# A first mixture of experts that scatters one row per token and choice, with its later batches normalised in the next stage, and more products without use ahead of four attention stages

## The chip, the cores and the metric

The program runs on one NeuronCore of a Trainium2 chip. The metric is the time of one execution on the device in microseconds (us). It is given as the median of several executions. One execution was also recorded by the profiler, and the times of single instructions come from that one.

## What is computed

The reference is a decoder of four layers (L0 to L3) over 8 sequences of 256 tokens with 128 features, all in float32. Each layer has three parts, a self attention or a scan (`a`), an attention against a context (`x`) and a feed-forward part (`f`). After each part comes `x = layernorm(x + part(x))`, without weights. The part that the change is mostly about is L0's feed-forward part, a mixture of 8 experts in which every token picks two:

```
probs = softmax(xf @ Wg);  vals, idx = top_k(probs, 2)
w = vals / (sum(vals) + 1e-9)
for k in range(2):
    oh  = one_hot(idx[:, k], 8)
    pos = cumsum(oh, axis=0) - 1 + counts;  keep = (oh == 1) & (pos < 256)
    counts += sum(keep);  combine += w[:, k] * keep
out = sum over e of combine[:, e] * (gelu(xf @ W1[e] + b1[e]) @ W2[e] + b2[e])
```

Each expert takes at most 256 token choices, so there are 8 x 256 = 2048 slots for 4096 choices (2048 tokens, two choices each), and what finds no slot is dropped.

## The kernel before

Twelve stages run one after another in the order L0a, L0x, L0f, L1a, L1x, L1f, L2a, L2x, L2f, L3a, L3x, L3f. In every stage each engine (PE = TensorE, DVE = VectorE, ACT = ScalarE, POOL = GpSimd, SP = the queue of plain DMAs) has its own hand-written program. There is no planner: each engine walks the steps of a stage in a fixed order, and semaphores tie the engines together, so an instruction that waits holds back everything behind it on its engine. The activations stay in `x_tok` (128 lanes x 16 tiles x 128 features, two tiles per batch). The semaphore `x_done` counts the batches that are normalised, and the next stage starts on a batch when it is counted. The weights of a stage are loaded by SP when the stage before it has begun. `due(g, offset, per)` tells in which steps which batch is served.

**L0f, routing** (`L0f` of the vector engine, from L2761). The logits are in PSUM. DVE finds the first and second choice in the helper `choose` (L2775 to L2780), which compares with the maximum, multiplies by the weights `w8` of the experts, takes the maximum again and compares again. PE counts the choices ahead of each token with two products (L1484, L1485). DVE copies the counts (L2802), runs a running sum over them (L2803) and gets each choice's place in its expert. It then forms two 0/1 tables, `whose` (L2812, L2813) and `hot` (32 instructions, L2815). PE multiplies the tables (L1490, 32 products), which gives the token of every slot. Before DVE turns that into row numbers `slot_of` (L2825 to L2829), it computes the two shares of each token (L2820 to L2823).

**L0f, experts.** SP has written every batch of `x_tok` to two tensors in device memory, `x_rows` (to read from) and `sum_rows` (to add to). For each expert `e`, POOL gathers its 2 x 128 rows into `big` with two indirect DMAs (`gather`, L849). PE transposes them (`turn_slots`, L1507), multiplies by W1 (`first_layer`, L1515), ACT takes the gelu (L2156), PE multiplies by W2 (`second_layer`, L1530, L1532) and DVE scales each row by its share into `V` (`copy_y`, L2859). POOL then adds the rows to `sum_rows` with two accumulating indirect DMAs (`add_rows`, L858). An expert's add waits until that of the expert before has landed, since two experts can add to one row:

```
def add_rows(e):
    pool.wait_ge(sem(f"{n}_copied"), y_copied(e))
    if e:
        pool.wait_ge(sem(f"{n}_added"), 32 * e)
```

POOL's order is gather 0, 1, 2, 3, then add 0, gather 4, add 1, gather 5, add 2, gather 6, add 3, gather 7, add 4, 5, 6, 7. Empty slots point behind the 2048 rows: a gather leaves them out, and an add puts them into rows that nobody reads.

**L0f, end.** When all has landed, SP reads the 2048 sums back (L628, four tiles first), and DVE and POOL normalise all eight batches: `deviations` (L2874 to L2879), POOL's power for the inverse root (L873), `normed` (L2885). In L1a, PE's first step then transposes batch 0 (`turn_x`, L972) and after it computes `fold` (L957, 8 products of weights), which ACT copies (L1928). Then come V (`project_v`, L987, four chunks a batch), q and k (`project`, L1003), their rotation by DVE (L2421, L2423) and POOL (L789, L793) and the scores (L1015 to L1019). L1a has 8 heads x 8 batches = 64 steps, from step -5 on.

**The four other attention stages with 16 heads that are not clipped** (L1x, L2x, L2f, L3x; `turned_stage`) take 8 pairs of heads per batch. Their steps begin at g = -8 (L2x: -18). Before step 0, PE turns and projects the first batch and spreads the heads (`unit`, L1182). `stream_on(bank, times)` (L1351) issues products of the identity with a constant mask, of 128x128 by 128x256 in bf16, whose results are never read. They stand behind the odd steps before 0 (4 each) and behind the steps 0 to 7 (4 each; L3x only from step 3). `project_v(0)` stands at step -1.

**Constants.** POOL builds the masks of later stages in `later_consts` (L660 to L673), at the start of its L0f.

## Time and profile before

| what | value |
|---|---|
| median of 3 executions | 1880.15 us (1878.22 to 1899.85) |
| the profiled execution | 1880.75 us |
| its span, first to last instruction | 1879.0 us |
| PE busy | 1567.0 us (83%), 12643 instructions |
| DVE busy | 1290.6 us (69%), 2887 instructions |
| ACT busy | 1055.7 us (56%), 2176 instructions |
| POOL busy | 658.6 us (35%), 741 instructions |
| the chain that ended last, by engine | PE 45%, DVE 23%, POOL 10%, issue 10%, ACT 9%, DMA 2% |
| mean granted clock of PE | 0.895 of full speed |

The span is the time between the first and the last recorded instruction, and 1.75 us of the execution lie outside it. The busy times count an engine's instructions, without those that only wait or issue a plain DMA. "Issue" in the chain is time in which an engine waited for nothing that the profile shows. The granted clock is the share of TensorE's full speed that the chip let it have.

### The profile page before, as it was taken

To read this page: it belongs to the slowest core of one execution; us is meant where nothing else is said; L and a number is where in the kernel's file an instruction comes from. 1 tells how busy PE (TensorE), PEld (TensorE's weight loads), DVE (VectorE), ACT (ScalarE), POOL (GpSimd) and SP (SyncE) were. 2 spreads that over 40 slices of the span, in tenths; PEclk is the share of its full clock that TensorE was granted. 3 is DMA by queue.
4 is the path that set the end of the run, shared out by engine and by line. 5 is a ranking of instruction groups with operands and counts; after the bars stand their busy time and mean duration, and the time that the engine had idled before them with its cause. 6 is when DMAs were issued, how large, how long until landed. Compare 5 with 4: busy or idle time off the path is not lost.

```text
span 1879.0 us, 34275 instructions
## 1 busy us (share of the span) xinstructions
PE 1567.0 (83%) x12643; PEld 1117.1 (59%) x12646; DVE 1290.6 (69%) x2887; ACT 1055.7 (56%) x2176; POOL 658.6 (35%) x741
## 2 busy tenths in 40 slices
PE   6488856599997888879988899888899988978875
PEld 5344435378876555757777666555569955645542
DVE  2678862377776886579999577648844465358877
ACT  4388842176774675378787155537744440037755
POOL 1355536488884022435667223220000010001223
PEclk9699978799998899968888899999989997769985
DMA  2200121200000000000000100000000000000000
GB/s 95 108 13 13 34 86 31 45 1 1 2 1 1 2 2 2 4 34 1 1 1 1 54 2 2 2 12 1 2 2 1 1 9 1 0 18 2 2 1 23
DMA packets 13607, 28.84 MB, mean 15 GB/s; under 512 B 1505, under 2 KB 10113, under 8 KB 12545
## 3 DMA queue, kind: packets, MB, share of 16 engines
q1 hardware_dynamic: 10626, 24.55, 3.7%
q0 software_dynamic: 2816, 2.10, 0.8%
q8 instruction: 103, 1.69, 0.4%
q14 instruction: 62, 0.51, 0.1%
HBM read 21.38 MB, written 5.24 MB: 14 GB/s over the span
## 4 chain that ended last, share of the span: by engine, by line
PE 45%; DVE 23%; POOL 10%; issue 10%; ACT 9%; DMA 2%; SPq 0%; DVEq 0%; POOLq 0%; ACTq 0%
PE PS L1269 5%; DVE negmax L2504 4%; PE PS L1329 4%; POOL big L793 3%; PE PS L1562 3%; PE PS L1573 3%; DVE V L3059 3%; POOL big L781 3%; ACT big L2030 2%; ACT big L2008 2%; PE PS L1808 2%; POOL big L789 2%; PE PS L1351 2%; PE PS L1799 2%; PE PS L1274 2%
## 5 line engine op out<-in xcount | busy, mean ns | idle before, releaser
L2008 ACT ACTIVATE big<-PS 128x1024 f32<-128x1024 f32 (+1 forms) x256 | 248.4, 971 | 165.6 <-PE PS L1280 164.7
L2504 DVE TENSOR_REDUCE negmax<-PS 128x4 f32<-128x1024 f32 x192 | 235.0, 1224 | 65.9 <-PE PS L1269 64.8
L677 POOL TENSOR_TENSOR rstd<-veps,mhalf 128x2 f32<-128x2 f32 x72 | 51.8, 719 | 419.9 <-DVE veps L2392 419.5
L1269 PE MATMUL PS<-KS,QS 32*128 32x256 f32 (+1 forms) x1152 | 137.0, 324 | 54.5 <-DVE negmax L2504 40.1
L1269 PEld LDWEIGHTS PS<-KS,QS 32*128 32x128 f32 x1152 | 89.2, 192 | 133.1 <-DVE negmax L2504 92.3
L1280 PE MATMUL PS<-QS,KS 32*128 32x256 f32 (+1 forms) x1152 | 134.6, 321 | 1.4 <-ACT big L2008 1.4
L1329 PE MATMUL PS<-big,V 128*32 128x256 f32 (+1 forms) x2048 | 134.5, 381 | 0.7 <-ACT big L2008 0.4
L703 POOL TENSOR_TENSOR res<-resb,XB 128x256 f32<-128x256 f32 x24 | 17.4, 726 | 283.4 <-ACT resb L2094 283.4
L2523 DVE SCALAR_TENSOR_TENSOR QT<-PS,wint 128x1024 f32<-128x1024 f32 x64 | 77.2, 1218 | 30.1 <-PE PS L1222 30.0
L745 POOL TENSOR_SCALAR KT<-QT 128x1024 f32<-128x1024 f32 x64 | 66.7, 1042 | 68.9 <-DVE QT L2523 67.0
L1280 PEld LDWEIGHTS PS<-QS,KS 32*128 32x128 f32 x1152 | 85.2, 188 | 5.7 <-issue 3.9
L2171 ACT ACTIVATE QT<-PS,W 128x256 f32<-128x256 f32 x128 | 53.8, 471 | 60.5 <-PE PS L1562 60.5
L1325 PE MATMUL PS<-big,V 128*32 128x512 f32 x512 | 67.9, 651 | 20.9 <-ACT big L2030 11.6
L781 POOL TENSOR_SCALAR big<-big,rsum 128x256 f32<-128x256 f32 (+1 forms) x144 | 60.6, 435 | 68.9 <-DVE rsum L2439 68.9
L1708 PE MATMUL PS<-OT,SEL 16*128 16x256 f32 x256 | 72.4, 427 | 13.5 <-DVE V L3063 13.5
L793 POOL TENSOR_TENSOR big<-big 128x512 f32<-128x512 f32 x64 | 81.3, 1270 | 5.0
L1724 PE MATMUL PS<-On,V 128*128 128x128 f32 x512 | 82.0, 327 | 0.0
L2250 ACT ACTIVATE QT<-x_tok,rt 128x128 f32<-128x128 f32 x256 | 77.8, 386 | 6.9 <-PE PS L1695 4.4
L1724 PEld LDWEIGHTS PS<-On,V 128*128 128x128 f32 x512 | 75.8, 235 | 9.3 <-issue 9.2
L1329 PEld LDWEIGHTS PS<-big,V 128*32 128x32 f32 x2048 | 54.5, 111 | 45.1 <-issue 15.7
L2030 ACT ACTIVATE big<-KT,W 128x1024 f32<-128x1024 f32 x64 | 73.2, 1144 | 8.6 <-POOL KT L745 8.6
L1003 PE MATMUL PS<-OT,W 128*128 128x256 f32 x272 | 72.9, 389 | 2.4 <-ACT QT L1967 2.4
(442 smaller groups left out, 4301.6 us busy)
## 6 DMA issues: line engine op xcount, KB each, us to landing
W<-in_wpack SPq DMA_DIRECT2D x1, 4180.0 KB, 12.3
W<-in_wpack SPq DMA_DIRECT2D x1, 2560.0 KB, 8.7
W<-in_wpack SPq DMA_DIRECT2D x1, 2449.5 KB, 8.3
masks<-in_mask SPq DMA_DIRECT2D x8, 256.0 KB, 2.8
W<-in_wpack SPq DMA_DIRECT2D x1, 1538.0 KB, 6.2
x_tok<-in_x SPq DMA_DIRECT2D x1, 1024.0 KB, 4.8
ctxT<-in_ctx SPq DMA_DIRECT2D x1, 1024.0 KB, 5.9
sum_rows<-ctxT SPq DMA_DIRECT2D x1, 1024.0 KB, 4.1
```

Of the source, the lines that this page charges most:

```text
L781: ins = nc.gpsimd.tensor_scalar(PRW[:, u % 4, c0:c1], PRW[:, u % 4, c0:c1], rsum[:, u % 16, j:j + 1], 1.0, ALU.mult, ALU.mult)
L793: nc.gpsimd.tensor_tensor(q, q, RTW[:, u % 4, :, :], ALU.add).then_inc(sem("t_rope"), 1)
L1003: mm = nc.tensor.matmul(PS[:, QKB[u % 2], k * S:(k + 1) * S], w(f"{n}_w{x}", h * P, (h + 1) * P), OT[:, b, :], start=True, stop=True)
L1269: mm = nc.tensor.matmul(PS[:, MAXB[half], o], QS[r, bm % 2, tm, j * P:(j + 1) * P], KS[r, bm % 2, tm, k], start=not a.causal, stop=last)
L1280: mm = nc.tensor.matmul(PS[:, exp_banks(ge)[half], o], KS[r, be % 2, te, kb * P:(kb + 1) * P], QS[r, be % 2, te, q], start=not a.causal, s ...
L1329: mm = nc.tensor.matmul(out_rows[:, skip:S], v, PX[:, T % 2, h, kb * S:(kb + 1) * S - skip], start=first, stop=last)
L1724: mm = nc.tensor.matmul(PS[:, YB, j * P:(j + 1) * P], chunk("h", t)[:, at:at + P], by_state[:, 4 * c + k, :], start=False, stop=c == 3 and ...
L2008: nc.scalar.activation(PX[:, T % 2, 2 * p:2 * p + 2, 0:cols], PS[:, exp_banks(g)[0]:exp_banks(g)[0] + 2, 0:cols], ACT.Exp, scale=a.scale). ...
L2030: nc.scalar.activation((PX, PX2)[k][:, T % 2, 2 * p:2 * p + 2, :], clipped((QT, KT)[k], g), ACT.Exp, scale=a.scale, bias=w(("high_base", " ...
L2250: ins = nc.scalar.activation(chunk("x", t)[:, at:at + P], x_tok[:, 2 * b + j, :], ACT.Copy, scale=B_cols(b)[:, i:i + 1])
L2504: ins = nc.vector.tensor_reduce(negmax[:, h:h + 2, :].rearrange("p h j -> p (h j)"), banks.rearrange("p h (j k) -> p (h j) k", j=2), AX.X, ...
L2523: nc.vector.scalar_tensor_tensor(clipped(QT, g), PS[:, pair_banks(g):pair_banks(g) + 2, :], -100.0 / a.scale, capT[:, g // PAIRS % 2, :].u ...
```

## The change

The change does the following.

1. **Routing.** In the first choice the compare and the multiplication by `w8` become one instruction on the shifted logits. The copy of the counts (L2802) goes: PE writes them in the order in which the running sum reads them from PSUM. The second half of `whose` is formed by ACT. `slot_of` comes from two instructions, ahead of the four that compute the shares. A slot now holds a choice's number (tile, lane and which choice, 0 to 4095), and an empty slot holds 4096 or more.
2. **Scatters.** `x_rows` and the new `y_rows` have 4096 rows, `x_tok` is written to both halves of `x_rows`, and SP fills `y_rows` with zeros in L0a. `scatter` is a plain indirect DMA with a bounds check, without the wait for the expert before.
3. **Sums on chip.** SP reads both halves of `y_rows` back, two tiles of each first, then fourteen of each. POOL adds them batch by batch, all eight in L0f, and DVE adds `x_tok`.
4. **Later batches.** L0f normalises batch 0 only. Batches 1 to 7 are normalised by DVE and POOL in L1a at the steps -5, -3, -1, 1, 3, 5 and 7 and the step behind each.
5. **L1a's start.** `fold` stands ahead of `turn_x(0)` and waits for the last scatter. 12 products without use follow it.
6. **Other stages.** More products without use in L1x, L2x, L2f and L3x, and `project_v(0)` at step 0.
7. **Constants.** `later_consts` runs at the start of the program.

The diff, cut to its core:

```
-                    sp.wait_ge(ctx_loaded, 16)
-                    sp.dma_start(sum_rows[B * S:B * S + E * CAPACITY, :]..., ctxT[:, :])
+                    sp.wait_ge(consts, EARLY)
+                    sp.dma_start(y_rows.rearrange(...), zeros.unsqueeze(1).broadcast_to([P, 8, 512])).then_inc(sem("L0f_rows"), 16)
...
                     sp.wait_ge(sem("L0f_added"), 32 * E)
-                    for k, (a, b) in enumerate(((0, 4), (4, NT))):
-                        sp.dma_start(summed_in[:, a:b, :], by_lane[1][:, a:b, :])
+                    for k, (a, b) in enumerate(((0, 2), (2, NT))):
+                        sp.dma_start(y_first[:, a:b, :], y_half[0][:, a:b, :]).then_inc(sem(f"L0f_back{k}"), 16)
+                        sp.dma_start(y_second[:, a:b, :], y_half[1][:, a:b, :]).then_inc(sem(f"L0f_back{k}"), 16)
...
+            later_consts()
...
                 for s in range(W_X_AT, H * B + W_LAST):
+                    if n == "L1a" and (b := rows_due(s)) is not None:
+                        root_of_rows(b)
                     if 0 <= s - 1 < H * B:
                         norm(s - 1)
...
-                def add_rows(e):
+                def scatter(e):
                     pool.wait_ge(sem(f"{n}_copied"), y_copied(e))
-                    if e:
-                        pool.wait_ge(sem(f"{n}_added"), 32 * e)
                     for j in range(2):
-                        nc.gpsimd.indirect_dma_start(sum_rows, ..., slot_y(e)[:, j * P:(j + 1) * P], None, compute_op=ALU.add)
+                        nc.gpsimd.indirect_dma_start(y_rows, ..., slot_y(e)[:, j * P:(j + 1) * P], None,
+                                                     bounds_check=2 * B * S - 1, oob_is_err=False).then_inc(sem(f"{n}_added"), 16)
+
+                def both_choices(b):
+                    if b < 2:
+                        pool.wait_ge(sem(f"{n}_back{b}"), 32)
+                    y = y_first[:, 2 * b:2 * b + 2, :]
+                    nc.gpsimd.tensor_tensor(y, y, y_second[:, 2 * b:2 * b + 2, :], ALU.add).then_inc(sem(f"{n}_placed"), 1)
-                later_consts()
...
+                for b in range(B):
+                    both_choices(b)
+                    if b == 0:
+                        root_of_rows(b)
...
+                    if s == W_X_AT and not first:
+                        pe.wait_ge(sem("L0f_added"), 32 * E)
+                        fold()
+                        for _ in range(12):
+                            nc.tensor.matmul(PS[:, YB, 0:S], identb[:, :], causal[:, 0, :], start=True, stop=True)
                     if (b := due(s, W_X_AT, H)) is not None:
                         turn_x(b)
-                    if s == W_X_AT:
+                    if s == W_X_AT and first:
                         fold()
...
-                        if (b := due(g, a.v_at)) is not None:
+                        if (b := due(g, a.v_at)) is not None and (b or a.clip):
                             project_v(b)
...
+                        if g == 0:
+                            project_v(0)
                     if not a.clip:
                         if g < 0:
-                            stream_on(MAXB[0], 4 * (g % 2))
+                            stream_on(MAXB[0], {-7: 14, -5: 10, -3: 10, -1: 4}.get(g, 6 * (g % 2)))
+                        elif g < 4:
+                            stream_on(EXPB[0], 8)
...
-                            if n != "L3x" or g >= 3:
-                                stream_on(OUTB, 4)
+                            if g >= 4:
+                                stream_on(OUTB, 5)
...
+                act.wait_ge(sem(f"{n}_slots"), 2)
+                nc.scalar.activation(whose[:, :, 1, :], in_chunk, ACT.Copy, scale=route("lane")).then_inc(sem(f"{n}_lg"), 1)
...
                     if (b := due(s, H + W_Y_AT, H)) is not None:
                         normalise(n, b, line, (res, resb)[b % 2])
+                    if n == "L1a":
+                        if (b := rows_due(s)) is not None:
+                            moments_of_rows(b)
+                        if (b := rows_due(s - 1)) is not None:
+                            normalise_rows(b)
                     if not first and 0 <= s + 2 < H * B:
                         rotate(s + 2)
...
+                ch.step(nc.vector.scalar_tensor_tensor(found, rt[:, 0, :, :], 0.0, w8, ALU.is_equal, ALU.mult))
+                ch.step(choose(0))
...
-                ch.step(nc.vector.tensor_copy(by_expert(cnt), PS[:, 1, 0:S].rearrange("p (c e) -> p e c", e=E)))
-                ch.step(nc.vector.tensor_tensor_scan(pre, keep_on, cnt, 0.0, ALU.mult, ALU.add))
+                ch.step(nc.vector.tensor_tensor_scan(pre, keep_on, PS[:, 1, 0:S], 0.0, ALU.mult, ALU.add))
...
                 ch.step(nc.vector.tensor_tensor(prob, prob, wide(rts[:, 1, :]), ALU.mult))
+                dve.wait_ge(sem(f"{n}_counts"), 2)
+                ch.step(nc.vector.tensor_scalar(slot_share, PS[:, 7, 16:32], 2.0 * B * S, None, ALU.add))
+                nc.vector.tensor_tensor(slot_of[:, :], PS[:, 7, 0:16], slot_share, ALU.add).then_inc(sem(f"{n}_placed"), 1)
                 for k in range(2):
                     ch.step(nc.vector.tensor_tensor(scaled, prob, ohb[:, k, :, :], ALU.mult))
                     ch.step(nc.vector.tensor_reduce(rts[:, 2 + k, :], scaled, AX.X, ALU.add))
...
+            def moments_of_rows(b):
+                both_tiles = slice(2 * b, 2 * b + 2)
+                dve.wait_ge(sem("L0f_placed"), 2 + b)
+                line.step(nc.vector.tensor_tensor(y_first[:, both_tiles, :], y_first[:, both_tiles, :], x_tok[:, both_tiles, :], ALU.add))
+                for t in (2 * b, 2 * b + 1):
+                    line.did(nc.vector.bn_stats(stats_of[:, t, :], y_first[:, t, :]))
...
+            def normalise_rows(b):
+                dve.wait_ge(sem("rstd"), before("L0f", "rstd") + b + 1)
```

## Rows read from the trace of the kernel before

**Rows 1.** Chain of waits from 262 to 372 us: shares by line of this stretch.

```profile
by line: issue 26.8%; DMA sum_rows<-V,slot_of 15.6%; POOL sum_rows L858 11.1%; POOL big L849 10.0%; PE PS L987 5.0%; DVE big L2815 4.7%; PE PS L957 3.1%; DMA big<-sum_rows 2.6%; DVE x_tok L2397 1.7%; PE PS L1003 1.6%; ACT W L1928 1.0%; PE P
```

**Rows 2.** Timeline of the routing: start us, length us, engine, line, operation, out and in.

```profile
268.37 0.63 POOL L669 TENSOR_SCALAR_AFFINE_SELECT causal<-causal 128x512 bf16<-128x512 bf16 x1
268.51 0.63 DVE L2777 TENSOR_TENSOR rt<-rt,W 128x128 f32<-128x128 f32 x1
...
270.86 0.29 DVE L2777 TENSOR_TENSOR rt<-rt,W 128x128 f32<-128x128 f32 x1
...
272.56 0.42 DVE L2802 COPY big<-PS 128x256 f32<-128x256 f32 x1 [0.29 <-PE PS L1485]
...
282.76 0.40 PE L1490 MATMUL PS<-big 128*128 128x32 bf16 x8 [0.90 <-DVE big L2815]
...
284.81 0.18 DVE L2829 SCALAR_TENSOR_TENSOR slot_of<-one_more 128x16 int32<-128x16 f32 x1
```

**Rows 3.** Groups by form, 150 to 420 us: busy us, mean ns | idle before.

```profile
L858 POOL DMA_INDIRECT sum_rows<-V,slot_of x16 | 25.4, 1585 | 19.0 <-DMA sum_rows<-V,slot_of 8.2 <-DVE V L2859 7.1 <-issue 3.7
L849 POOL DMA_INDIRECT big<-x_rows,slot_of x16 | 17.0, 1064 | 21.1 <-DVE slot_of L2829 16.5 <-issue 4.3 <-DMA sum_rows<-V,slot_of 0.3
...
L694 POOL TENSOR_TENSOR XB<-x_tok,W 128x256 f32<-128x256 f32 x6 | 4.4, 733 | 0.1
```

**Rows 4.** Timeline of the experts: first result, last gather, last result.

```profile
302.86 0.61 DVE L2859 TENSOR_SCALAR V<-PS,one_more 128x128 f32<-128x128 f32 x2
...
328.53 1.04 POOL L849 DMA_INDIRECT big<-x_rows,slot_of  x1 [0.31 <-issue]
...
342.16 0.61 DVE L2859 TENSOR_SCALAR V<-PS,one_more 128x128 f32<-128x128 f32 x2 [2.39 <-PE PS L1532]
```

**Rows 5.** Pieces of the chain of waits, 262 to 372 us: start us, us, what.

```profile
350.34 3.24 DMA sum_rows<-V,slot_of
353.59 2.82 DMA big<-sum_rows
...
359.60 3.43 PE PS L957 x16
...
364.18 2.09 PE PS L987 x2
```

**Rows 6.** Timeline of L1a's start: batch 0 normalised, first rotation, first scores.

```profile
358.25 0.60 DVE L2885 TENSOR_SCALAR x_tok<-big,rt 128x128 f32<-128x128 f32 x2
...
370.91 0.69 DVE L2421 TENSOR_TENSOR big<-PS,W 128x512 f32<-128x512 f32 x1 [2.15 <-PE PS L1003]
...
375.72 0.28 PE L1015 MATMUL PS<-causal,identb 128*128 128x256 bf16 x1 [0.85 <-POOL big L793]
```

**Rows 7.** Windows: length, busy PE, PEld, DVE, ACT, POOL, granted clock, DMA share, GB/s.

```profile
440.00:467.00 27.00, 25.92 (x176) 21.73 (x176) 20.02 (x56) 19.03 (x62) 22.70 (x34) 1.00 0.00 1
610.00:615.00 5.00, 4.65 (x34) 2.83 (x35) 2.46 (x6) 2.64 (x5) 0.00 (x0) 0.50 0.00 0
1065.00:1070.00 5.00, 5.00 (x16) 3.45 (x15) 0.49 (x2) 1.20 (x3) 1.41 (x2) 0.50 0.01 3
1250.00:1255.00 5.00, 5.00 (x22) 3.24 (x21) 2.56 (x4) 0.37 (x1) 0.00 (x0) 0.50 0.00 0
1675.00:1680.00 5.00, 4.64 (x34) 2.79 (x32) 2.38 (x5) 2.29 (x3) 0.00 (x0) 0.50 0.01 3
```

**Rows 8.** Timeline of PE at the starts of L1x, L2x and L3x.

```profile
593.74 0.74 PE L1182 MATMUL PS<-HL,spread_by 32*128 32x256 f32 x8 [1.51 <-DVE HL L2562]
...
618.02 1.07 PE L1329 MATMUL PS<-big,V 128*32 128x256 f32 x16
...
1060.30 0.73 PE L1182 MATMUL PS<-HL,spread_by 32*128 32x256 f32 x8 [3.80 <-DVE QT L2584]
...
1655.88 0.73 PE L1182 MATMUL PS<-HL,spread_by 32*128 32x256 f32 x8 [1.19 <-DVE HL L2562]
...
1685.85 1.07 PE L1329 MATMUL PS<-big,V 128*32 128x256 f32 x16
```

**Rows 9.** Piece of the chain of waits, 1044 to 1075 us: products without use at half clock.

```profile
1069.36 0.85 PE PS L1351 x4
```

137 lines of the change are left out of this document (65 added, 72 removed).

## The prediction

> **What bounds the kernel now.** I read the page first: PE is busy for 83% of the span, but over stages with different limits, so I went by stretches. The chain of waits over L0f and the start of L1a [rows 1] shows what ends last there. PE has under 10% of it; 27% is issue, 16% the landing of accumulating DMAs, 21% POOL's issue of indirect DMAs. This stretch is latency: from the routing's first rows to the first scores of L1a it is 107 us [rows 2, 6]. The windows show the second thing: at the start of L1x, L2x, L2f and L3x PE is busy and runs at half clock (0.50) [rows 7], while the other engines are half idle. Everything else is left as it is by the change.
>
> **Routing.** The first choice's multiplication took 0.63 us, beside a mask instruction of POOL, and the same line took 0.29 for the second choice [rows 2]. The mask work moves to the program's start, where POOL is idle, and the multiplication is merged with its compare: -0.5 us. The copy of the counts goes: 0.42 and 0.04 until the next [rows 2], -0.46. ACT takes the second half of `whose`, some 0.26 of DVE's time. `slot_of` ends at 284.99 now; the tables' products end at 283.16 [rows 2], and with two instructions of 0.2 behind them it would be there at 283.6: -1.4. Sum: -2.6 us.
>
> **Scatters.** Now the chain goes expert by expert. POOL spends 1585 ns on an add and 1064 ns on a gather, with 0.30 between [rows 3], so a round of two adds and two gathers lasts 6.5 us; the last gather is issued at 329.57 and the last result is in `V` at 342.77, 13.2 us behind it [rows 4]. From expert 4 on each add waits for the landing of the one before (8.2 us in all [rows 3]). The last add is issued at 350.34 and has landed at 353.59 [rows 5]. The trace has no plain scatter. Upper bound: POOL's time of an add, 1.585. Then the last gather ends 2.6 earlier (327.0), the last result is there at 340.2, scatter 6 ends at 341, and the second of scatter 7 starts at 343.0 and lands at 346.2: -7.4 with the routing. Lower bound: a gather's 1.06, the nearest row, since it moves the same 128 rows of 512 bytes with a bounds check and without arithmetic. Then a round lasts 2 x 1.35 + 2 x 1.38 + 0.3 = 5.75 us. The first result is in V at 300.9 (302.86 + 0.61 - 2.6 [rows 4]), four rounds end at 324.1, the last result is there at 337.3, and the second scatter starts at 338.8 and lands at 342.0: -11.6. I take -11.6, with -7.4 as the other end.
>
> The Trainium skill ("DMA: Bandwidth & Descriptors", SWDGE vs HWDGE) says that GpSimd builds one pair of descriptors, read and write, per DMA operation. By that rule direction alone would not make a scatter dearer than a gather, which is the -11.6; by the row of the add it is -7.4.
>
> **Sums and batch 0.** The first read back took 2.82 us for 256 KB [rows 5]; two of 128 KB should take about as long. New on batch 0's path are POOL's add (a 128x256 addition is 733 ns [rows 3]) and DVE's add of x, some 0.4: +1.15 us. Batch 0 would be normalised at 358.85 [rows 6] - 11.6 + 1.15 = 348.4: -10.4. The zeros go out at 9 us, behind the loads, and nothing waits for them for 280 us: 0. The second copy of x takes the place of the writes to `sum_rows`: 0.
>
> **L1a's start.** `fold` stands between batch 0 and its V now, so the first V product starts 5.3 us behind batch 0 [rows 5, 6]. Of those, 3.43 are the fold and 1.15 ACT's copy of it. After the change both run during the read back, with the 12 products behind them: 4.6 us. A V product takes 2.09 us at half clock [rows 5], and three of them at full clock are worth another 3.1. If nothing else held it, L1a would gain 7.7 us. But something does. On DVE the first rotation now starts 12.1 us behind batch 0 and the first scores follow 4.8 us later [rows 6], and until then DVE had time for all batches. After the change DVE's first rotation stands behind batches 1 and 2, and their normalisation behind POOL's inverse root, which stands behind POOL's seven additions (7 x 0.76 = 5.3 us). Worked through: additions done 5 to 6 us behind batch 0, batch 1 normalised at 6.2 to 7.4, batch 2's moments at 8.8, its root at 9.6, normalised at 10.2, first rotation at about 10.3 and first scores at 15. That is 2 us less than the 16.9 now. Then batches 3 to 7 put 2.0 us of DVE work into every second step. In steady state DVE's 56 instructions in 27 us are eight steps with one batch's end [rows 7], so a pair of steps has 6.75 us and DVE is busy for 5.0 of them. With 2.0 more it is at 7.0: just over the period, some 0.3 us per pair, and 1 to 2 us in all where PE's early steps without values are shorter. What is gained at the front is so given back within eight steps. I take 0 for L1a from batch 0 on, between -7.7 (all of fold and clock) and +12 (C below).
>
> A rule of the skill speaks against the change here. "SBUF — State Buffer", Who interferes with whom: a DVE instruction with two SBUF inputs contends with a GpSimd instruction that reads SBUF, and who comes first holds the port for the whole instruction. The 0.63 beside POOL against 0.29 alone agrees. By the rule each of DVE's seven new additions can wait for a POOL instruction.
>
> **Products without use.** The clock is at half in all four windows [rows 7]. Four such products take 0.85 us there [rows 9], 0.21 each, and half of that at full clock. Before step 0 there are 38 instead of 16, 22 more. At full clock they are 2.4 us, and in L1x they fit where PE waits anyway (1.51 us ahead of the first `unit` [rows 8], and 0.7 behind each of two further ones). At steps 0 to 3 there are 4 more each, 0.9 us over what the waits hide, and `project_v(0)` behind the first scores gives 0.8 back. If the clock then stays up:
> L1x: from the first `unit` to the first values 593.74 to 618.02, 24.3 us [rows 8], of which four steps ran at half clock and took 10.6 us; at full clock a step is 1.9: -2.8, with the products -2.4.
> L2f: three steps at half clock, -1.8.
> L3x: 1655.88 to 1685.85, 30.0 us [rows 8]. It would be like L1x without its slow steps, 22 us: -7.5. It starts with a cold PE, on which 14 products are 2 to 3 us instead of 1.2 us of waiting, so -6.
> L2x: its clock falls in a gap of 3.80 us on DVE [rows 8], of which the products fill 1.1. Ten further products before step -7 lengthen the path by 0.9. If the clock stays up, -0.8 in the sum; if it falls all the same, +4. I take 0.
> Sum: -10.2 us, with bounds of -13 and +18 (below).
>
> **The sum** is made against the profiled execution, 1880.75 us, of which 1.75 are outside the span: -10.4 (L0f) + 0 (L1a) - 10.2 (four stages) = -20.6, so 1860 us. The median of the runs is 0.6 us below the profiled one, and I leave it at 1860. The kernel's time can be told apart from no change from about 2% on, 38 us: this gain of 1.1% is within that.
>
> **Rivals.**
> A. The plain scatter costs POOL what the add did: 4.2 us less gained, 1864. For it: both go from SBUF to device memory. Against: arithmetic and read of the target go.
> B. The clock falls in the four stages all the same, since the gaps are caused by DVE and ACT and the heads are spread by products on 32 rows only. The gain of 10.2 is gone and the products that no gap hides cost about 2: 1872. For it: the clock fell in L1x although PE was busy for most of that stretch.
> C. The later batches stall L1a. DVE waits in order for POOL's root, POOL waits in order for DVE's moments, and both contend for SBUF. Nothing of 7 x 2.0 = 14 us is hidden then, 2 us of the front remain: 1872.
> D. The other side, one mechanism: the products run at half clock and don't raise it. There are 42 more in L1x and in L2f, 54 in L3x, 51 in L2x, 189 x 0.21 = 40 us on PE, which issues in order. Waits hide at most 22 us, so +18 against -10.4: 1888. It decides from the point at which what the waits don't hide exceeds 10.4 us, about 155 products at half clock. Against it: full bf16 products are what PE did at full clock elsewhere, and 14 at a time leave little gap.
> E. L1a's front keeps all of its 7.7 us and L2x's clock stays up: 1851.
>
> **How the numbers follow.** Forecast 0.45 (1854 to 1866 by itself), A 0.15, B 0.15, C 0.10, D 0.03, E 0.12. B and C end near 1872, and both in part are likelier than one in full, so the range is 1848 to 1874. It leaves out D, B with C together and the fast tail. Faster by over 2% (below 1843) needs more than all bounds give at once (10.4 + 7.7 + 13 = 31): 0.03. Slower by over 2% needs twice D: 0.01. Within 2%: 0.96.
>
> **What would show it.** The scatters on POOL: 1.0 to 1.1 us each if the lower bound holds, 1.5 or more for A. No POOL wait on a DMA of the expert before. Last scatter landed at 340 to 344 and batch 0 normalised near 348. In L1a: PE at clock 1.00 when V starts, DVE's first rotation near 10 us behind batch 0 (15 would be C), and DVE idle before `normalise_rows` with POOL's root as the releaser. In the stages: granted clock 1.00 in the first 25 us of L1x, L2f and L3x, and 22 to 24 us from the first `unit` to the first values of L3x. The prediction is wrong if the clock rows stay at 0.50, or if L1a's length from batch 0 on changes by more than 5 us.

## The result, and the profile of the changed kernel

| what | before | changed |
|---|---|---|
| median of 13 executions each | 1880.66 us (1870.60 to 1899.85) | 1872.18 us (1865.47 to 1884.25) |
| ratio | | 0.9944, 95% interval 0.9924 to 0.9964 |
| the profiled execution | 1880.75 us | 1869.56 us |
| mean granted clock of PE | 0.895 | 0.905 |

The ratio is taken over the fast executions of both kernels, the medians over all. By the ratio the changed kernel is faster by 0.56% (0.45% by the medians), and the interval leaves out 1. The forecast of 1860 us is 12 us too low: of the 20.6 us only 8.5 came in the medians and 11.2 in the profiled executions.

The chain of waits of the changed kernel from 343 to 372 us (start us, length us, what) shows what stands behind the last scatter now, where [rows 5] had one read back and `fold`:

```profile
343.56 2.27 DMA y_rows<-V,slot_of
...
347.29 8.46 DMA big<-y_rows
...
355.83 3.04 POOL KT L876 x5
...
359.44 1.40 POOL KT L876 x2
360.84 0.67 POOL rt L893
```

The last scatter has landed at 345.83, where the last add had landed at 353.59 [rows 5]: -7.8 us. Behind it stands something that the chain of before did not have: 8.46 us in which fourteen tiles of both halves are read back, and then POOL's seven additions. This is no longer batch 0's path but that of batches 1 to 7.

The groups of POOL between 300 and 346 us answer to [rows 3] (busy us, mean ns | idle before):

```profile
L868 POOL DMA_INDIRECT y_rows<-V,slot_of x16 | 16.0, 998 | 25.1 <-DVE V L2901 19.4 <-issue 3.0 <-DVE On L2891 2.7
L861 POOL DMA_INDIRECT big<-x_rows,slot_of x8 | 8.2, 1025 | 2.4 <-issue 2.4
```

A plain scatter takes 998 ns, a gather 1025 ns here, and no scatter waits for a DMA of the expert before. The timeline of DVE and POOL (start us, length us) answers to [rows 6]:

```profile
351.72 0.60 DVE L2931 TENSOR_SCALAR x_tok<-KT,rt 128x128 f32<-128x128 f32 x2 [0.83 <-POOL rt L893]
356.69 0.83 DVE L2918 TENSOR_TENSOR KT<-KT,x_tok 128x256 f32<-128x256 f32 x1 [4.37 <-POOL KT L876]
...
361.53 0.60 DVE L2931 TENSOR_SCALAR x_tok<-KT,rt 128x128 f32<-128x128 f32 x2 [2.71 <-POOL rt L893]
...
364.27 0.60 DVE L2931 TENSOR_SCALAR x_tok<-KT,rt 128x128 f32<-128x128 f32 x2 [0.80 <-POOL rt L893]
364.79 0.68 DVE L2459 TENSOR_TENSOR big<-PS,W 128x512 f32<-128x512 f32 x1
```

Batch 0 is normalised at 352.32 (351.72 + 0.60), batches 1 and 2 at 362.13 and 364.87, and only then comes the first rotation. And the windows of the stages' starts, as in [rows 7] (the granted clock is the third number from the end):

```profile
610.00:615.00 5.00, 4.59 (x56) 3.12 (x57) 4.15 (x9) 2.82 (x5) 0.00 (x0) 1.00 0.00 0
1065.00:1070.00 5.00, 5.00 (x26) 3.72 (x25) 2.13 (x6) 0.37 (x1) 0.68 (x1) 0.50 0.00 0
1250.00:1255.00 5.00, 4.65 (x37) 3.29 (x35) 3.69 (x9) 0.99 (x3) 0.00 (x0) 1.00 0.00 0
1675.00:1680.00 5.00, 4.04 (x56) 2.51 (x56) 3.95 (x8) 3.64 (x6) 0.00 (x0) 1.00 0.01 3
```

In these windows PE runs at full clock in three of the four stages now; in L2x (1065 to 1070) it does not.

Since one execution differs from another in stretches that no edit touches, I compare stretches and not spans. The table has them for all profiled runs, each a difference of two times in the timelines. "Experts": from the first copy of a result into `V` to the last. "Scores": from `turn_x(0)` of L1a to its first scores (the product of q and k, 0.1 to 0.2 us behind the one with the mask). "Steps": from there to L1a's first batch being normalised. "Rest": from there to L1x's first `turn_x`. L1a as a whole is the sum of these three. The fronts go from a stage's first `turn_x` to its first `values`. "Other": the sum of all stretches between the fronts and to the last product.

| run | experts | scores | steps | rest | L1x | L2x | L2f | L3x | other |
|---|---|---|---|---|---|---|---|---|---|
| before | 39.3 | 16.9 | 39.2 | 174.7 | 28.3 | 41.9 | 27.5 | 35.3 | 1148.5 |
| changed | 41.8 | 17.1 | 44.2 | 173.9 | 25.6 | 46.2 | 25.5 | 28.6 | 1146.9 |
| e12, changed again | 40.0 | 17.0 | 44.3 | 174.1 | 25.6 | 43.0 | 25.5 | 28.4 | 1153.7 |
| e1, L0f part only | 35.7 | 16.7 | 44.2 | 173.9 | 28.4 | 41.4 | 31.5 | 36.2 | 1142.7 |
| e2, products only | 41.5 | 16.6 | 39.2 | 174.4 | 25.6 | 42.9 | 25.5 | 28.7 | 1138.3 |
| e3 | 35.5 | 9.6 | 43.6 | 179.6 | 25.6 | 41.5 | 25.5 | 28.7 | 1144.7 |
| e4 | 35.6 | 12.2 | 45.0 | 174.9 | 25.6 | 41.4 | 25.5 | 28.3 | 1146.5 |
| e5 | 35.6 | 9.6 | 42.5 | 179.8 | 25.6 | 41.5 | 25.5 | 28.6 | 1144.9 |
| e6 | 37.1 | 9.6 | 42.7 | 180.3 | 25.6 | 41.5 | 25.5 | 28.7 | 1146.0 |
| e7 | 35.7 | 13.0 | 42.7 | 181.2 | 25.6 | 46.3 | 25.5 | 28.7 | 1145.7 |
| e8 | 35.6 | 25.5 | 40.6 | 174.5 | 25.6 | 46.3 | 25.5 | 28.3 | 1151.6 |
| e9 | 35.5 | 16.6 | 45.2 | 167.2 | 25.6 | 40.1 | 25.5 | 28.3 | 1151.6 |
| e10 | 35.5 | 9.6 | 45.1 | 172.9 | 25.6 | 41.5 | 25.5 | 28.7 | 1145.7 |
| e11 | 35.4 | 12.2 | 46.0 | 167.2 | 25.6 | 40.1 | 25.5 | 28.3 | 1151.6 |

The last column holds nothing that the runs change on purpose, and it moves by 15 us between them. Much of that goes with the clock: the stretch from L2f's first `values` to L3x's first `turn_x` takes 369 us at a mean granted clock of 0.95 (e7) and 389 us at 0.90 (e12). So a median of a few runs says little on 5 us, and a stretch says much.

Two things must be kept apart from what an edit does. The medians of the kernel before, taken beside the runs, are 1880.8 us for e1 to e4, 1888.7 for e5 to e8, 1888.1 for e9 to e11 and 1884.5 for e12, so across these groups only the ratios can be compared. And in all variants of the changed kernel but e12 the experts take 35 to 37 us instead of 41.8, which makes their profiled execution shorter by 5 to 6 us whatever was edited in L1a.

### The profile page after: what moved, and what is told of

The parts are those of the page before. It is cut to its first block, busy times and chain, and to the rows that moved or that the text cites. A ratio compares the mean times of both kernels' runs of the same rounds, so it can differ in the third digit from the quotient of the medians.

```text
span 1867.8 us, 34707 instructions
## 1 busy us (share of the span) xinstructions
PE 1581.1 (85%) x12844; PEld 1135.7 (61%) x12847; DVE 1295.2 (69%) x2889; ACT 1055.6 (57%) x2177; POOL 651.8 (35%) x750
## 4 chain that ended last, share of the span: by engine, by line
PE 47%; DVE 23%; POOL 11%; issue 9%; ACT 8%; DMA 2%; SPq 0%; DVEq 0%; POOLq 0%; ACTq 0%
PE PS L1294 5%; PE PS L1354 4%; DVE negmax L2547 4%; POOL big L803 4%; DVE V L3099 3%; PE PS L1596 3%; PE PS L1607 3%; POOL big L791 3%; PE PS L1376 3%; ACT big L2066 2%; POOL big L799 2%; PE PS L1299 2%; ACT big L2044 2%; PE PS L1350 2%; PE PS L1368 2%
## 5 line engine op out<-in xcount | busy, mean ns | idle before, releaser
L1294 PE MATMUL PS<-KS,QS 32*128 32x256 f32 (+1 forms) x1152 | 135.4, 320 | 50.3 <-DVE negmax L2547 37.1
L1354 PE MATMUL PS<-big,V 128*32 128x256 f32 (+1 forms) x2048 | 139.1, 392 | 0.7 <-ACT big L2044 0.4
L1758 PE MATMUL PS<-On,V 128*128 128x128 f32 x512 | 89.8, 348 | 0.8 <-DVE V L3103 0.8
L1758 PEld LDWEIGHTS PS<-On,V 128*128 128x128 f32 x512 | 83.3, 255 | 10.3 <-issue 9.3
L1376 PE MATMUL PS<-causal,identb 128*128 128x256 bf16 x595 | 85.9, 287 | 0.0
L1350 PE MATMUL PS<-big,V 128*32 128x512 f32 x512 | 67.7, 649 | 20.9 <-ACT big L2066 11.6
L1742 PE MATMUL PS<-OT,SEL 16*128 16x256 f32 x256 | 70.5, 418 | 11.6 <-DVE V L3103 11.6
```

The source lines that it names most:

```text
L1294: mm = nc.tensor.matmul(PS[:, MAXB[half], o], QS[r, bm % 2, tm, j * P:(j + 1) * P], KS[r, bm % 2, tm, k], start=not a.causal, stop=last)
L1350: mm = nc.tensor.matmul(out_rows.rearrange("p (k c) -> p k c", k=2), v, PX_BOTH[:, :, T % 2, h, kb * S:(kb + 1) * S], start=first, stop=last)
L1354: mm = nc.tensor.matmul(out_rows[:, skip:S], v, PX[:, T % 2, h, kb * S:(kb + 1) * S - skip], start=first, stop=last)
L1376: nc.tensor.matmul(PS[:, bank, 0:S], identb[:, :], causal[:, 0, :], start=True, stop=True)
L1758: mm = nc.tensor.matmul(PS[:, YB, j * P:(j + 1) * P], chunk("h", t)[:, at:at + P], by_state[:, 4 * c + k, :], start=False, stop=c == 3 and ...
```

## The experiments

### The two halves of the change

e1 takes the products and `project_v` of the four stages back, e2 puts only them into the kernel before:

```
-                        if g < 0:
-                            stream_on(MAXB[0], {-7: 14, -5: 10, -3: 10, -1: 4}.get(g, 6 * (g % 2)))
-                        elif g < 4:
-                            stream_on(EXPB[0], 8)
+                        if g < 0:
+                            stream_on(MAXB[0], 4 * (g % 2))
```

> The changed kernel with the products without use and project_v(0) as in the kernel before. Theory (the L0f part nets nothing: it gains 6.5 us until batch 0 is normalised and loses 5 us from there to L1a's steady steps): 1879 to 1881 us, L1a's first batch normalised at 413 to 414 us in the trace, the front of L1x back at 28 us and of L3x at 34 to 36 us. Rival (the L0f part is worth what was forecast for it, about 10 us, and the products nothing): 1870 us. A second rival is that the clock's later dips move the end by 5 us either way whatever is changed; then this run and the next do not add up to the whole change.

> The kernel before with only the products without use and project_v(0) of the change. Theory (all of the gain is theirs: -2.7 in L1x, -1.8 in L2f, -6.6 in L3x, +4.3 in L2x, and what later dips give): 1870 to 1873 us; front of L1x (first transposition to first values) 25 to 26 us against 28.3, of L3x 28 to 29 against 35.3, of L2x 46 against 41.9. Rival (they are worth nothing by themselves and the L0f part brings the gain): 1880 us with the fronts at their old lengths.

e1: median 1875.0 us, ratio 0.9952 (0.9896 to 1.0007). e2: median 1872.9 us, ratio 0.9925 (0.9868 to 0.9982); one of its six executions took 3532.7 us, and the ratio leaves it out. The intervals cannot part the theory from its rival for e1, but the stretches can. With the products taken back, L1x's front is at 28.4 and L3x's at 36.2 us again; with them alone these are 25.6 and 28.7. The gain in the fronts of L1x, L2f and L3x is the products'. L1a's steps take 44.2 us in e1 and 39.2 in e2, as in the changed kernel and in the one before: the 5 us lost there belong to the L0f part. My first theory for e1, that the L0f part nets nothing, was too low: the experts take 35.7 us in e1 and not 41.8. The ratios of the two halves, 0.48% and 0.75% of gain, add up to more than the 0.56% of the whole, as the second rival of e1 had it: the experts and L2x's front are both at their long values in the changed kernel.

### L1a's start: which work stands ahead of the first rotation

e3 does the later batches once in eight steps, both additions on DVE, from a tile that L1a leaves alone:

```
 def rows_due(s):
-    b, rest = divmod(s - W_X_AT, 2)
-    return b + 1 if rest == 0 and b + 1 < B else None
+    b, rest = divmod(s, 8)
+    return b + 1 if s >= 0 and rest == 0 and b + 1 < B else None
...
-                for b in range(B):
-                    both_choices(b)
-                    if b == 0:
-                        root_of_rows(b)
+                both_choices(0)
+                root_of_rows(0)
```

> The changed kernel, but batches 1 to 7 are added up, and normalised, once in eight steps of L1a (moments at the steps 0, 8, 16 up to 48), both additions on DVE, with the second choice's rows read back to a tile that L1a does not use; POOL adds for batch 0 alone. Theory (L1a lost its lead since batch 1 waits for 8.5 us of read back and DVE's first rotation stands behind batches 1 and 2, and then POOL and DVE contend): first rotation 5 to 7 us behind batch 0 instead of 12.5, first scores 10 to 12 behind it instead of 16.9, L1a's first batch normalised 6 to 8 us earlier than in the changed kernel (405 to 408), and 1863 to 1867 us. Rival (V's start on PE and ACT bounds the front, not the rows): first scores still 15 or more behind batch 0, time as the changed kernel's 1872.

Median 1858.5 us, ratio 0.9898 (0.9846 to 0.9950). The timeline of e3, DVE and then PE:

```profile
347.28 0.60 DVE L2933 TENSOR_SCALAR x_tok<-KT,rt 128x128 f32<-128x128 f32 x2 [0.90 <-POOL rt L891]
352.89 0.69 DVE L2457 TENSOR_TENSOR big<-PS,W 128x512 f32<-128x512 f32 x1 [5.00 <-PE PS L1021]
...
356.25 1.39 DVE L2917 TENSOR_TENSOR KT<-KT,QS 128x256 f32<-128x256 f32 x1
```

```profile
357.41 0.28 PE L1033 MATMUL PS<-causal,identb 128*128 128x256 bf16 x1 [0.93 <-POOL big L803]
```

The first rotation waits for PE's q and k and for nothing else, and it starts 5.0 us behind batch 0; the first scores come at 9.6 instead of 17.1. L1a's first batch is normalised 53.2 us behind batch 0 and not 61.2. The theory holds for the front. But it left out the other side: a round of eight steps now takes 27.6 us instead of 26.45, and of the 7.5 us gained at the front L1a's rest gives 5.7 back. L1a as a whole is 2.4 us shorter than in the changed kernel; most of e3's gain in time is in the experts (6.3) and in L2x's front (4.7).

e4 leaves the work where the change put it and only lets it start earlier: the read back in parts of two, four and ten tiles, POOL's additions one at a time behind its roots.

```
-                    for k, (a, b) in enumerate(((0, 2), (2, NT))):
+                    for k, (a, b) in enumerate(((0, 2), (2, 6), (6, NT))):
```

> The changed kernel, but the read back goes in three parts (two, four, ten tiles of each half), POOL adds batches 0, 1 and 2 ahead of L1a and the others behind its inverse roots in L1a, one at a time. Batches are normalised at the same steps as in the changed kernel. Theory (what holds the front is the 8.5 us of read back, then POOL's seven additions in a row ahead of the first root): second read back landed 3 to 4 us behind its issue, batch 1 normalised at 355 to 357 instead of 361.5, first rotation 8 to 9 us behind batch 0 instead of 12.5, L1a's first batch normalised 3 to 4 us earlier, 1868 us. Rival (DVE's own work for batches 1 and 2 beside POOL is what holds it): first rotation 11 or more behind batch 0 and no gain.

Median 1863.3 us, ratio 0.9900 (0.9853 to 0.9947). The chain of e4:

```profile
344.89 0.72 POOL rt L897
345.61 1.40 POOL KT L893 x2
347.00 0.42 DVE KT L2922
```

POOL adds batches 1 and 2 right behind batch 0's root, 10.2 us earlier than in the changed kernel (355.83), of which 6.0 are the scatters' earlier landing. The first rotation starts 7.7 us behind batch 0, the first scores come at 12.2 instead of 17.1. So 4.9 of the 7.5 us that e3 gains at the front were the waiting for fourteen tiles and the seven additions in a row; e4 changes both at once and does not tell them apart. The timeline of DVE in e4 shows what is left:

```profile
354.79 0.69 DVE L2463 TENSOR_TENSOR big<-PS,W 128x512 f32<-128x512 f32 x1 [1.74 <-PE PS L1027]
```

The rotation waits 1.74 us for PE's q and k; the first V product took 2.05 us in this run, at half clock, in spite of the 12 products. DVE's rows are not what ends this wait any more.

e8 goes the other way and normalises all eight batches in L0f, as the kernel before did:

```
                 moments_of_rows(0)
                 normalise_rows(0)
+                for b in range(1, B + 1):
+                    if b < B:
+                        moments_of_rows(b)
+                    if b > 1:
+                        normalise_rows(b - 1)
```

> The changed kernel, but all eight batches are normalised in L0f, as in the kernel before, and none in L1a. Theory (moving the later batches into L1a was not what cost; the late read back and DVE's work ahead of the first rotation were, and here all of that work stands ahead of it): first rotation 17 to 20 us behind batch 0, first scores 22 to 25, L1a's first batch normalised 62 to 64 us behind batch 0 (the changed kernel 61.9, before 56.8), time 1872 to 1876. Rival (the move itself costs, through POOL's roots and DVE's port in the first steps): 57 to 59 us and 1868.

Median 1873.2 us, ratio 0.9924 (0.9889 to 0.9960). First scores 25.5 us behind batch 0, L1a's first batch 66.2 behind it, more than expected. The whole of L1a (scores, steps, rest) takes 240.6 us against 235.1 in the changed kernel and 230.8 before. The move into L1a was right: with these sums on chip it saves 5 us. What costs is that the sums are there so late.

e8 also helps to find the 5.0 us that L1a's steps lost. PE's timelines have them at one place, between the first scores and the fifth:

| | first to fifth scores | fifth to thirteenth |
|---|---|---|
| before | 11.7 us | 25.8 us |
| changed (and e1, e12) | 16.7 us | 25.9 us |
| e8 | 13.2 us | 25.8 us |

From the first rotation to the fifth scores the windows are, before and changed (busy PE, PEld, DVE, ACT, POOL):

```profile
370.91:387.40 16.49, 13.73 (x72) 9.49 (x71) 13.53 (x32) 11.66 (x34) 12.70 (x18) 0.98 0.03 10
364.79:385.90 21.11, 13.26 (x65) 9.69 (x65) 19.85 (x57) 10.94 (x33) 14.89 (x21) 0.84 0.01 2
```

DVE is busy for 19.85 of 21.11 us in the changed kernel, against 13.53 of 16.49 before, and POOL waits for it (changed kernel, POOL):

```profile
377.46 0.84 POOL L791 TENSOR_SCALAR big<-big,rsum 128x128 f32<-128x128 f32 x2 [1.64 <-DVE rsum L2477]
```

In this stretch stand the moments of batches 3, 4 and 5. Batches 6 and 7 come behind the fifth scores, beside steps of 3.5 us with a V product on PE, and there the moments and roots cost 0.1 us in eight steps. Without later batches in L1a (e8) the first stretch is 3.4 us shorter than in the changed kernel. What makes up the other 1.5 us against the kernel before is not shown. The clock may have a part: it is granted at 0.84 in this stretch against 0.98 before, though PE is busy for only 13.26 of the 21.11 us.

e7 takes the 12 products behind `fold` away (from e5, which is shown below):

```
                         fold()
-                        for _ in range(12):
-                            nc.tensor.matmul(PS[:, YB, 0:S], identb[:, :], causal[:, 0, :], start=True, stop=True)
```

> e5_late_gap without the 12 products behind fold at L1a's start. Theory (fold alone does not bring the clock up before V starts): a V product 2.1 us instead of 1.1, first rotation 7 to 8 us behind batch 0 instead of 5, first scores 12 to 13 instead of 9.6, +2 to +3 us. Rival (fold's 3.8 us of work bring the clock up anyway, or q and k and not V set the first rotation): first scores at 10 or less and the same time as e5_late_gap.

Median 1869.8 us, ratio 0.9884 (0.9806 to 0.9961). V's first product takes 2.05 us at half clock instead of 1.10, the first rotation comes at 8.0 and the first scores at 13.0. The prediction's 3.1 us for V at full clock is right in size: 3.4 at the scores. The products don't always bring it: of the eleven profiles that have them, V's first product is at 1.10 in eight and at 1.92 to 2.05 in e4, e9 and e11.

### What sets L1a's pace

e5 moves the moments of the later batches into the gap of DVE ahead of L1a's own normalise:

```
+                    if n == "L1a" and (b := rows_due(s)) is not None:
+                        moments_of_rows(b)
                     if (b := due(s, H + W_Y_AT, H)) is not None:
                         normalise(n, b, line, (res, resb)[b % 2])
```

> e3_late_rows with the rows' moments moved: for batches 2 to 7 they stand at the steps 4, 12, 20 up to 44 ahead of L1a's own normalise, where DVE waits 2.6 us for POOL's root in every round of eight steps; POOL's root for the rows comes one step and the normalisation two steps later. Theory (each round of eight steps with rows costs 27.6 us in e3_late_rows against 26.45 without, since DVE sets the pace; in the gap the rows' 2.4 us cost little): rounds of L1a at 26.5 to 26.9 us, L1a 3 to 5 us shorter than in e3_late_rows, first scores still 9.6 behind batch 0, 1853 to 1856 us. Rival (what lengthens the round is POOL, with one more root and the shared port): rounds stay at 27.3 or more and the time stays at 1858.

Median 1862.7 us, ratio 0.9879 (0.9826 to 0.9932). The rounds stayed at 27.6 us, and the timeline of POOL in e5 shows why:

```profile
411.95 0.83 POOL L791 TENSOR_SCALAR big<-big,rsum 128x128 f32<-128x128 f32 x2 [3.06 <-DVE rsum L2475]
412.75 0.64 POOL L799 TENSOR_TENSOR big<-QT,W 128x256 f32<-128x256 f32 x1
413.46 1.27 POOL L803 TENSOR_TENSOR big<-big 128x512 f32<-128x512 f32 x1
414.69 0.70 POOL L891 TENSOR_TENSOR rt<-rt,mhalf 128x2 f32<-128x2 f32 x1
415.38 0.83 POOL L791 TENSOR_SCALAR big<-big,rsum 128x128 f32<-128x128 f32 x2
416.17 0.64 POOL L799 TENSOR_TENSOR big<-QT,W 128x256 f32<-128x256 f32 x1
...
421.46 0.83 POOL L791 TENSOR_SCALAR big<-big,rsum 128x128 f32<-128x128 f32 x2
...
424.23 0.83 POOL L791 TENSOR_SCALAR big<-big,rsum 128x128 f32<-128x128 f32 x2
```

In the steps without a V product POOL works with nothing between, 2.77 us each (421.46 to 424.23), so a root for the later batches, 0.70, makes such a round longer. That is 0.70 of its 1.2 us; where the rest comes from is not shown. Once a round it stands still for 3.06 us, since DVE waits for L1a's own root, which POOL has behind a step's work, and POOL then waits for DVE. Eight steps, the root and the stall are 8 x 2.76 + 0.70 + 3.06 = 25.8 of the 26.45 us that a round takes without later batches. My theory had DVE set the pace of these rounds, and it fell; that POOL does was only argued so far.

So e9, e10 and e11, whose edit is no part of the change, let DVE take L1a's own normalise one step later, on the changed kernel, on e5 and on e4:

```
-                    if (b := due(s, H + W_Y_AT, H)) is not None:
+                    if (b := due(s - 1, H + W_Y_AT, H)) is not None:
                         normalise(n, b, line, (res, resb)[b % 2])
```

(batch 7 stays at its step)

> The changed kernel with one edit in L1a, not part of the change: DVE takes L1a's own normalise of batches 0 to 6 one step later. In e5_late_gap a round of eight steps stayed at 27.4 us although DVE's work was in its gap, and POOL works 2.76 us a step back to back, except for 3.06 us once a round: it waits for a reciprocal of DVE, which waits 2.6 us for POOL's root. Theory (POOL, with this stall, sets L1a's pace; the forecast took DVE): rounds of 23.3 to 24.5 us instead of 26.45, L1a 14 to 22 us shorter, 1850 to 1858 us. Rival (PE, busy for 26 of 27 us in a round, sets the pace): 25.8 us a round or more, under 5 us in all.

> e5_late_gap (rows once in eight steps, both additions on DVE) with the same later normalise of L1a's own batches. Theory (POOL sets the pace; its root for the rows is 0.7 us a round, and DVE's work for the rows delays POOL only where POOL waits for DVE): rounds of 24 to 25 us instead of 27.4, first scores 9.6 us behind batch 0 as before, L1a 27 us shorter than in the changed kernel, 1840 to 1847 us. Rival (DVE's 2.4 us a round become the bound once the stall is gone): rounds of 26 us or more, 1850 or more.

> e4_split (rows at the steps -5 to 8, additions on POOL) with the same later normalise of L1a's own batches. Theory (the two gains are in different stretches and add up): first scores 12.2 us behind batch 0, rounds of 23.3 to 24.5 us, 1841 to 1848 us. Rival (PE sets the pace at about 26 us a round): 1862 as e4_split.

| run | round of 8 steps | median | ratio, 95% interval |
|---|---|---|---|
| e9 | 25.7 us | 1856.1 us | 0.9828 (0.9785 to 0.9871) |
| e10 | 27.4 us | 1853.8 us | 0.9838 (0.9784 to 0.9892) |
| e11 | 25.7 us | 1858.7 us | 0.9850 (0.9802 to 0.9899) |

The stall of 3.06 us is gone in e9, but a round became shorter by 0.7 us and not by 2 to 3. The window of one round of e9:

```profile
432.70:458.40 25.70, 25.02 (x172) 21.23 (x170) 20.12 (x57) 18.77 (x62) 22.23 (x33) 1.00 0.00 1
```

PE is busy for 25.0 of the 25.7 us, and a timeline of POOL in e9 shows that it now waits in the steps in which DVE, for its part, waits up to 1.08 us for PE's scores:

```profile
440.08 0.83 POOL L791 TENSOR_SCALAR big<-big,rsum 128x128 f32<-128x128 f32 x2 [0.65 <-DVE rsum L2477]
...
443.59 0.82 POOL L791 TENSOR_SCALAR big<-big,rsum 128x128 f32<-128x128 f32 x2 [0.73 <-DVE rsum L2477]
...
447.09 0.82 POOL L791 TENSOR_SCALAR big<-big,rsum 128x128 f32<-128x128 f32 x2 [0.74 <-DVE rsum L2477]
```

Those steps take 3.5 us each and are the ones with a V product on PE. The rival of e9 is nearer: POOL's stall was worth 0.7 us a round, and what is left is close to PE's busy time. L1a as a whole is 6.2 us shorter; its last round, which has no full set of steps, alone became 2.5 us shorter (14.4 against 16.9). In e10 the rival is right too. The round stays at 27.4 us although the same edit is in it: POOL still waits 2.84 us once a round, behind 0.84 for its root, and DVE, with the later batches' work, runs without a gap there. In e11 both gains add up: scores 12.2, rest 167.2, and L1a in all 225.4 us against 235.1 in the changed kernel. Its time, 1858.7 us, still misses the theory's 1841 to 1848, since the rounds did. e9 to e11 are faster than both kernels by the intervals; among themselves they are not told apart. Their gain is not all of this edit: e9's profile has 6.3 us less in the experts and 6.1 us less in L2x's front than that of the changed kernel.

### The experts and PE's clock

e6 puts ten products ahead of each wait for a gather from expert 4 on, in e5:

```
                 def turn_slots(e):
+                    if e >= 4:
+                        for _ in range(10):
+                            nc.tensor.matmul(PS[:, (2, 6)[e % 2], 0:S], identb[:, :], causal[:, 0, :], start=True, stop=True)
                     pe.wait_ge(*rows_in(e))
```

> e5_late_gap with 10 products without use on PE ahead of each wait for a gather from expert 4 on (40 in all). Theory (the changed kernel's last result came 41.8 us behind the first since PE fell to half clock behind a 2.4 us wait for a gather, and 35.5 where it did not; the products fill the wait): 35.5 to 37.5 us from the first to the last result in V, never 41, and the slowest runs of this kernel come closer to its median. Median 0 to 2 us below e5_late_gap. Rival (the products lengthen PE's path, which sets this phase, by what no wait hides, up to 4.3 us): 38 us or more with the clock at full, median 2 to 3 us above e5_late_gap.

Median 1870.7 us, ratio 0.9936 (0.9899 to 0.9973). Experts 37.1 us at full clock, 1.5 more than without the products. The clock does not fall there without them either, in the nine other runs with this L0f code, so in the profile they only cost. The rival is right in its sign. Its slowest of 12 executions is 1878.8 us, that of e5 1871.2 of six: nothing shows that they were steadied.

e12 runs the changed kernel once more:

> The changed kernel itself, unaltered, once more and with another profile. In its first profile PE fell to half clock among the experts (41.8 us from the first to the last result in V) and in L2x's front (46.2 us from the first transposition to the first values). Theory (these are chance of the single execution: the other kernels with the same code there showed 35.5 in seven of eight cases and 41.5 in six of eight): at least one of the two is short this time, 35.5 or 41.5; from batch 0 to the first scores 16.6 to 17.1 us and the fronts of L1x, L2f and L3x at 25.6, 25.5 and 28.5 again. Rival (they belong to this program's own timing): 41.8 and 46.2 again. The time: 1865 to 1875 us, a ratio to the kernel before of 0.988 to 0.996.

Median 1874.1 us, ratio 0.9960 (0.9934 to 0.9985). Neither side is right in full: experts 40.0 us, again with a fall of the clock, where nine of nine other runs have 35.4 to 35.7; L2x's front 43.0. In the changed kernel's timelines, DVE, then PE:

```profile
312.08 0.61 DVE L2901 TENSOR_SCALAR V<-PS,one_more 128x128 f32<-128x128 f32 x2 [4.08 <-remote]
```

```profile
315.70 2.00 PE L1549 MATMUL PS<-On,W 128*128 128x256 f32 x8
320.13 0.61 PE L1541 MATMUL PS<-W,big 128*128 128x128 f32 x2 [2.43 <-DMA big<-x_rows,slot_of]
320.53 1.92 PE L1564 MATMUL PS<-W,QT 128*128 128x128 f32 x8
...
325.83 3.78 PE L1549 MATMUL PS<-On,W 128*128 128x256 f32 x8
```

and in e10:

```profile
310.34 0.61 DVE L2902 TENSOR_SCALAR V<-PS,one_more 128x128 f32<-128x128 f32 x2 [2.39 <-PE PS L1564]
```

In the changed kernel DVE copies expert 2's result 1.74 us later than PE has it (312.08 against 310.34 in e10, whose experts began at the same 300.5); the profile names the releaser "remote", which stands for nothing that it recorded. The second profile has the same row with "remote", at 314.16. No other run has one. POOL's scatter is then late by as much, the gather behind it too, PE waits 2.43 us at 317.70, and from there it runs at half clock: eight products take 3.78 us and not 2.00. Two of two profiles against none of the other twelve, nine of them with the same code among the experts, speak for something of this program and against chance; what the 1.74 us are is open and wasn't tried. The clock can fall among the experts without it too: e2, with the L0f of the kernel before, has 41.5 us and a granted clock of 0.84 from 305 to 347 us, and no such row.

## Why the prediction was right or wrong

**Routing, forecast -2.6.** `slot_of` is formed at 281.28 instead of 284.81: -3.5, of which 2.3 are the instructions of the routing itself. The other 1.26 the forecast did not have. In the kernel before, the normalisation of L0x's last batch ran beside the first of POOL's mask instructions (timeline of before; the same of the changed kernel below it):

```profile
263.53 1.79 POOL L662 MEMSET SEL<- 16x2048 f32 x1
263.61 1.86 DVE L2397 TENSOR_SCALAR x_tok<-res,mv,rstd 128x128 f32<-128x128 f32 x2 [0.82 <-POOL rstd L677]
```

```profile
263.60 0.60 DVE L2435 TENSOR_SCALAR x_tok<-res,mv,rstd 128x128 f32<-128x128 f32 x2 [0.82 <-POOL rstd L687]
```

DVE's two instructions took 1.86 us beside a memset of 1.79, and 0.60 alone. e2, whose L0f is that of the kernel before, has the same pair, 1.86 beside 1.79.

**Scatters, forecast -11.6 with the routing.** The price was right: 998 ns at the lower bound of 1.06 us, with no wait for the expert before. Rival A falls. The prediction had taken from the Trainium skill ("DMA: Bandwidth & Descriptors", SWDGE vs HWDGE vs iDMA), which has one pair of descriptors for each DMA operation, that the direction alone would not make a scatter dearer, and 998 against 1025 ns agrees. The last landing came at 345.83 instead of 342.0. The step that fell short was "four rounds end at 324.1, the last result is there at 337.3": it took PE's work per expert at full clock. Where the clock held, in nine runs, the experts took 35.5 us, 3.8 less than before and 0.9 less than the forecast's 36.4 (300.9 to 337.3); in the changed kernel's own two profiles the late copy on DVE and the fall of the clock behind it took 4.5 to 6.3 us of that.

**Batch 0, forecast 6.4 us behind the landing.** It is 6.5. With the landing the gain up to there is 6.5 us instead of 10.4.

**L1a from batch 0 on, forecast 0.** It is +4.3 (235.1 against 230.8), and +4.5 in e12. This is the step that failed. Its two halves: "first scores at 15" is 17.1, since the forecast let the additions end 5 to 6 us behind batch 0 and gave the second read back no price. It took 8.46 us for fourteen tiles of two halves, and the additions ended 8.5 us behind batch 0 (360.83). e4 shows it: with smaller parts and the additions spread the scores are at 12.2. And "some 0.3 us per pair, and 1 to 2 us in all where PE's early steps without values are shorter" is 5.0 (44.2 against 39.2). The engine was named rightly and the place too, but not the size. The first four steps of the kernel before take 11.7 us, 2.9 each and not 3.4, so 2.0 us more of DVE's work in every second step do not fit, and DVE is busy for 19.85 of 21.11 us up to the fifth scores. Behind them, where the forecast had 0.3 us per pair, the later batches cost 0.1 in eight steps. Rival C, that the later batches stall L1a, had this mechanism at three times its price.

**Port.** DVE's addition for batch 1 takes 0.83 us beside POOL's additions and 0.43 alone, and in e3 one with two inputs in SBUF takes 1.39, while POOL has instructions of 1.26 and 0.82 running. This agrees with the rule of the Trainium skill ("SBUF — State Buffer", Who interferes with whom) that was weighed against the change. Its share in L1a's +4.3 was not measured by itself.

**Products, forecast -10.2.** L1x -2.7 (forecast -2.4), L2f -2.0 (-1.8), L3x -6.6 (-6), each within 0.4 us again in the eleven other profiles that have the products. L2x +4.3 (0), which is the forecast's own bound for a clock that falls all the same. Over the twelve profiles with the products L2x has 40.1 us in two (-1.8, the clock holds), 41.5 in five, 43 in two and 46.3 in three. Their mean is 42.7, 0.8 above before, so the forecast's 0 lay inside, and the changed kernel's first profile was near the bad end. In the two of 40.1 us the granted clock is 1.00 throughout the front; in those of 46.3 it is at 0.50 for more than six microseconds. Rivals B and D fall: three of four clocks are up, and no stage lost by the products what D said.

**The sum.** -6.5 + 4.3 - 2.7 + 4.3 - 2.0 - 6.6 = -9.2, and -1.6 in the other stretches, is -10.8 of the 11.2 us. Of the forecast's 20.6, 3.9 failed at the scatters, 4.3 in L1a and 4.3 in L2x; 1.1 came in over in the other three fronts and 2.0 outside of all steps, which leaves the 9.4 us that are missing.

**The range.** 1872.2 us lies within 1848 to 1874, but close to its end, and e12's 1874.1 lies at it. 1872 is also where rivals B and C each end, and neither came as priced: the clock rose in three of four stages, and L1a lost 4.3 us and not 12. The median is there because three misses of about 4 us each went the same way. Of the two signs that the prediction named against itself, one came in part (the clock row of L2x stayed at 0.50), the other nearly (L1a by 4.3 us, where more than 5 would have counted).

## What to carry to other kernels

Work moved off the critical path into the next stage has a price that depends on the steps in which it lands. Here batches 6 and 7 cost 0.1 us in all, in steps that a V product on PE made 3.5 us long; the batches in the first, short steps cost 3.4 of the 5.0 us, by e8, with DVE at 94% of its time; and once in eight steps (e3) each made a round 1.1 us longer. So the engine without a gap is to be looked for in the steps in which the work lands, and not in the average of a round. When data comes back in parts, make the second part small as well, and put what consumes it one at a time behind each part, since everything queued ahead of the next stage's first instruction counts.

## What the hardware showed that I had not expected

Two instructions of DVE that read and write SBUF took 1.86 us beside a memset of POOL and 0.60 alone, so a memset in another engine's queue stood on the critical path here. A plain indirect scatter from SBUF costs POOL 998 ns where an accumulating one cost 1585 [rows 3], and it lands 2.27 us behind its issue instead of 3.24. The fall of PE's clock to half among the experts came in both profiles of one program and in none of nine others with the same instructions there, behind a copy on DVE that began 1.74 us late for no recorded reason. And the unchanged stretches moved by 15 us between profiles, more than the whole gain.
